# A three-layer decoder block on one core: ScalarE scales and rounds two weights, VectorE only clips them, and all five instruction orders change

## What is computed

```python
# layer 1: four products with ternary weights and 8-bit activations
def _bitlinear(x, w):
    xn = _rmsnorm(x)
    s = 127.0 / clip(max(abs(xn)), 1e-05)
    xq = clip(round(xn * s), -128, 127) / s
    ws = 1.0 / clip(mean(abs(w)), 1e-05)
    wq = clip(round(w * ws), -1.0, 1.0) / ws
    return xq @ wq.T
f = sigmoid(_bitlinear(x, Wf))
i = silu(_bitlinear(x, Wi)) * (1 - f)
h = scan over the tokens of a sequence: h[t] = f[t] * h[t-1] + i[t]
o = _rmsnorm(_bitlinear(x, Wg)) * g_norm_weight * silu(h)
x = layernorm(x + _bitlinear(o, Wo))
# layer 2: each token goes to one of 4 experts by its id; all three weights are ctx[e]
y = (silu(x @ ctx[e].T) * (x @ ctx[e].T)) @ ctx[e].T
x = layernorm(x + y)
# layer 3
x = layernorm(x + x @ sum(factors) / sqrt(8) + bias)
```

## Time and profile before

| what | value |
|---|---|
| device time, three runs | 340.66, 343.01, 343.08 us; median 343.01 |
| the profiled execution | 342.06 us, of which the span from first to last instruction is 340.3 |
| busy over the span | PE 278.1 us (82%), PEld 211.9, DVE 226.3 (66%), ACT 229.6 (67%), POOL 190.8 (56%) |
| instructions | 5734 |
| moved by DMA | 37.02 MB, mean 109 GB/s |
| chain that ended last, by engine | PE 62%, ACT 9%, issue 5%, DVE 5%, DMA 2%, POOL 2% |

### The profile page before, as it was taken

The page is one execution under the profiler, slowest core; times in us unless marked ns, Lnnn a source line. Parts: engine busy times, 40 slices in busy tenths (PEclk is TensorE's granted clock), DMA queues, the critical chain, the costliest instruction groups (busy, mean ns, idle before and its releaser), DMA issues.

```text
span 340.3 us, 5734 instructions
## 1 busy us (share of the span) xinstructions
PE 278.1 (82%) x1505; PEld 211.9 (62%) x1518; DVE 226.3 (66%) x488; ACT 229.6 (67%) x456; POOL 190.8 (56%) x381
## 2 busy tenths in 40 slices
PE   1376646484879899999999998998999999999760
PEld 1253414252557678787778876676888888887540
DVE  2789999999987879968677696454543434543310
ACT  4687789889678769986887686476555644554530
POOL 2536765858637748865565856547444444454442
PEclk9999989879799999999999999999999999999975
DMA  7999981987593782013003002205111111000000
GB/s 233 387 388 387 225 196 62 185 153 143 130 227 79 115 179 65 1 62 126 0 33 141 17 15 111 62 7 186 56 40 56 62 66 62 33 26 29 4 6 0
DMA packets 17406, 37.02 MB, mean 109 GB/s; under 512 B 1503, under 2 KB 1631, under 8 KB 17376
## 3 DMA queue, kind: packets, MB, share of 16 engines
q0 software_dynamic: 6496, 15.74, 19.6%
q1 hardware_dynamic: 10880, 20.92, 19.2%
HBM read 26.68 MB, written 10.76 MB: 110 GB/s over the span
## 4 chain that ended last, share of the span: by engine, by line
PE 62%; ACT 9%; issue 5%; DVE 5%; DMA 2%; POOL 2%; ACTq 0%; POOLq 0%; DVEq 0%; SPq 0%
PE bank_y L1455 5%; PE bank_z L1455 5%; PE bank_y L1456 5%; PE bank_z L1456 5%; PE bank_z L1459 5%; PE bank_y L1459 5%; PE bank_m L1455 4%; PE bank_m L1456 4%; PE bank_m L1459 4%; PE bank_tr L1424 3%; PE bank_c L1357 2%; PE bank_q L1424 2%; PE bank_a L1357 1%; PE bank_b L1357 1%; DMA sorted_rows<-r,place 1%
## 5 line engine op out<-in xcount | busy, mean ns | idle before, releaser
L312 POOL TENSOR_SCALAR n_v<-n_dev 128x1 f32<-128x1 f32 (+1 forms) x46 | 8.8, 192 | 52.2 <-ACT x L644 26.7
L1455 PE MATMUL bank_y<-c_hi,h_hi 128*128 x76 | 31.8, 418 | 1.8 <-ACT h_hi L612 1.4
L996 DVE TENSOR_TENSOR act_z<-bank_z,act_z 128x512 f32<-128x512 f32 x19 | 13.1, 689 | 30.1 <-ACT act_z L626 30.1
L1455 PE MATMUL bank_m<-f_hi,m_hi 128*128 128x512 f32 x76 | 32.1, 423 | 0.8 <-ACT m_hi L612 0.8
L353 POOL TENSOR_TENSOR x<-x,bias_b 128x512 f32<-128x512 f32 x19 | 24.6, 1293 | 14.5 <-PE bank_q L1424 14.5
L1455 PE MATMUL bank_z<-c_hi,a_hi 128*128 x76 | 30.4, 400 | 2.8 <-ACT a_hi L612 1.5
L1456 PE MATMUL bank_m<-f_lo,m_hi 128*128 128x512 f32 x76 | 30.8, 405 | 0.0
L1456 PE MATMUL bank_y<-c_lo,h_hi 128*128 x76 | 30.1, 396 | 0.0
L1456 PE MATMUL bank_z<-c_lo,a_hi 128*128 x76 | 30.1, 395 | 0.0
L612 ACT ACTIVATE h_hi<-bank_tr 128x512 fp32r<-128x512 f32 x19 | 11.3, 596 | 26.7 <-PE bank_tr L1424 26.7
L313 POOL TENSOR_TENSOR n_d<-n_v,minus_half 128x1 f32<-128x1 f32 (+1 forms) x46 | 27.1, 588 | 3.8
(11 more groups left out here) (205 smaller groups left out, 848.7 us busy)
## 6 DMA issues: line engine op xcount, KB each, us to landing
f_sum<-in_factors POOLq DMA_DIRECT2D x7, 1024.0 KB
rows<-sorted_rows SPq DMA_DIRECT2D x19, 256.5 KB, 2.9
xs<-in_x SPq DMA_DIRECT2D x8, 512.0 KB, 7.6
c_stage<-in_ctx_t SPq DMA_DIRECT2D x4, 1024.0 KB, 14.3
sorted_rows<-pad_row SPq DMA_DIRECT2D x1, 1539.0 KB, 18.3
w_stage<-in_wf_t SPq DMA_DIRECT2D x1, 1024.0 KB, 8.7
w_stage<-in_wi_t SPq DMA_DIRECT2D x1, 1024.0 KB, 10.8
w_stage<-in_wg_t SPq DMA_DIRECT2D x1, 1024.0 KB, 13.0
```

Of the source, the lines that this page charges most:

```text
L996: v.tensor_tensor(act_z[:], bank_z[:], act_z[:], ALU.mult).then_inc(s.hid, 1)
L1455: t.matmul(bank[:], hi[:, c, :], w_hi(c), start=(c == 0), stop=False)
```

## The change

1. New scale_weights(m) on ScalarE: one pass of w_stage times the scale plus the rounding constant. New clip_weights(m) on VectorE: one instruction with minimum and maximum around that constant. They take the place of round_weights for W_G and W_O. W_F and W_I stay as they were.
2. The lists of calls of TensorE, VectorE, ScalarE and GpSimd are written in new orders, in the start, in the loop and in the prologue. SyncE's list is unchanged, and so are all other operations.

```diff
+                def scale_weights(m):
+                    act.wait_ge(s.wscale, 2 * m + 2)
+                    a.activation(w_stage[:, m, :], w_stage[:, m, :], ACT.Copy, bias=MAGIC, scale=w_scale[:, m:m + 1]
+                                 ).then_inc(s.wround_act, 1)
+
...
+                def clip_weights(m):
+                    dve.wait_ge(s.wround_act, m - W_I)
+                    v.tensor_scalar(w_stage[:, m, :], w_stage[:, m, :], MAGIC + 1.0, MAGIC - 1.0, ALU.min, ALU.max
+                                    ).then_inc(s.wclip, 1)
+
...
                 weight_total(W_I)
+                weight_total(W_G)
                 spread_max(0)
                 project_f(0)
-                weight_total(W_G)
-                weight_total(W_O)
...
                 silu_h_by_token(3)
+                transpose_a(0)
                 project_f(4)
-                transpose_a(0)
+                up(0)
                 project_i(4)
-                up(0)
+                transpose_h(0)
                 project_g(4)
-                transpose_h(0)
...
                     down(n - 1)
+                    mix(n - 3)
+                    transpose_a(n)
                     pe.wait_ge(s.xqt, min(g + 2, N_GROUPS))
                     transpose_m(n - 2)
                     if is_group(g + 1):
                         spread_max(g + 1)
-                    transpose_a(n)
-                    mix(n - 3)
                     up(n)
```

More of the change, by code:

```diff
@@ L717, in _ @@
-                silu_i(2, 0)
-                forget(2, 0)
-                silu_i(2, 1)
-                forget(2, 1)
-                o_by_channel(1)
-                high_of_ctx(2, range(2, 3))
-                max_row(3)
-                square_x(4, 1)
+                square_o(1, 0)
+                silu_i(2, 0)
+                square_o(1, 1)
+                square_g(2, 0)
+                high_of_ctx(1, range(2, 3))
+                silu_i(2, 1)
+                forget(2, 0)
+                norm_1(0)
@@ L725, in _ @@
+                square_x(4, 1)
+                square_g(2, 1)
+                max_row(3)
+                x_by_channel(3)
+                tanh_f(2, 1)
+                o_by_channel(1)
+                forget(2, 1)
+                high_of_ctx(1, range(3, 4))
+                high_of_ctx(2, range(0, 3))
+                silu_h(2, 0)
                 high_of_ctx(2, range(3, 4))
+                silu_h(2, 1)
                 high_of_ctx(3, range(0, 1))
-                silu_h(2, 0)
-                silu_h(2, 1)
+                square_1(1)
@@ L799, in _ @@
+                    square_2(n - 1)
+                    silu_z(n)
+                    o_by_channel(p)
+                    forget(g, 1)
+                    high_h(n)
+                    square_3(n - 2)
+                    silu_h(g, 0)
+                    norm_2(n - 1)
+                    high_a(n + 1)
+                    norm_3(n - 3)
+                    square_1(p)
                     if is_group(g + 1):
                         max_row(g + 1)
-                    tanh_f(g, 1)
-                    high_a(n)
@@ L1134, in _ @@
[L1134 to L1144 removed]
+                low_of_ctx([0])
+                output(0, 0)
+                output(0, 1)
+                low_of_ctx([1])
+                scale_x(2)
+                rescale_i(1, 0)
@@ L1145, in _ @@
+                max_o(0, 0)
+                max_o(0, 1)
+                quantise_x(2)
+                clip_weights(3)
+                rescale_i(1, 1)
+                weigh_g(1, 0)
+                quantise_o(0)
+                slot_offsets()
+                gate_i(1, 0)
+                max_x(3, 0)
+                scans(1, 0)
+                weigh_g(1, 1)
+                low_of_ctx([2])
+                gate_i(1, 1)
+                max_x(3, 1)
                 scans(1, 1)
                 rescale_f(2, 0)
+                residual_1(0)
```

395 lines of the change are left out of this document (180 added, 215 removed).

## The result

The changed kernel took 347.00 us (median of four; 346.95, 347.00, 347.00, 349.83) beside 342.41 for before (340.66 to 343.08): a ratio of 1.0195, interval [1.015, 1.024]. In a later session it gave 345.26 beside 341.48, 1.012 [1.009, 1.015]. So the change costs 1.2 to 2 per cent, 4 to 5 us, where the forecast said 341.7 with a range up to 344.7, and a loss of over one per cent had a chance of 0.09. What changed are the lists of four engines; SyncE's is as it was, though the title says five. The profiled execution has a span of 345.1 us where before had 340.3.

A forecast was written before the change was run, and what follows sets the result against it. It took VectorE to bound the kernel up to the first expert product at 97.19 us, TensorE after; -1.0 on VectorE and +0.65 on TensorE gave -0.35 from 342.06, so 341.7 us, range 338.8 to 344.7 including rivals.

The follow-up runs named there:

- e17: The kernel before with the new weight work, old orders, and three low_of_ctx moved from VectorE to GpSimd: 341.40 us beside 341.23 for before, ratio 1.0005.

## What to carry to other kernels

Where five hand-written lists have been fitted to each other, price an order by stretches, swapped on all engines at once: a single call moved on one engine of the loop cost 2 to 4 us a turn here, more than the whole difference between two complete orders. On an engine that idles 0.08 us in 85, go through its new list pair by pair and ask of every bank that is used twice what lies between, before asking about the feeders. And a busy share of 95 per cent is by itself no critical path: take something away (e17) before you book a saving.
